# Probabilities and values of an attention kernel as f16 pairs instead of float32r pairs

## The reference, cut to what matters

```python
q = (x @ Wq) ...                                   # 16 heads
k, v = jnp.split(x @ Wkv, 2, axis=-1)              # 4 groups
scores = jnp.einsum('brgtd,bgsd->brgts', qg, k) / jnp.sqrt(jnp.float32(HD))
scores = jnp.where(causal[None, None, None], scores + bias[None], -jnp.inf)
attn = jax.nn.softmax(scores, axis=-1)
out = jnp.einsum('brgts,bgsd->brgtd', attn, v)
return out @ Wo + bo
...
x = x + _L0_attn_ref(xn, ...) + _L0_ffn_ref(xn, ...)
```

## Time and profile before

| | |
|---|---|
| median of 3 runs | 1827.52 us (1823.84 to 1828.0) |
| profiled execution | 1826.36 us, of it the span of the profile 1824.5 us |
| granted TensorE clock, mean | 0.987 |
| TensorE busy | 1742.3 us, 95% |
| TensorE weight loads (beside the matmuls) | 959.6 us, 53% |
| VectorE busy | 1466.6 us, 80% |
| ScalarE busy | 990.1 us, 54% |
| GpSimd busy | 981.4 us, 54% |
| preamble: GpSimd's low parts of the query weights | 23.50 to 28.49 us |
| preamble: remainder of the first projection (L774) | starts 36.16 us |
| preamble: extra rows of the queries, stored by SyncE | 56.71 us |
| main loop: TensorE's first matmul | 116.83 us |
| main loop: ones of `vst` (L1257, two fills) | 124.12 us, 0.98 us |
| main loop: turn of the maxima in slot 3, ten heads apart | 435.62 and 1446.63 us, 101.1 us a head |

### The profile page before, as it was taken

The page is one execution under the profiler, slowest core; times in us unless marked ns, Lnnn a source line. Parts: engine busy times, 40 slices in busy tenths (PEclk is TensorE's granted clock), DMA queues, the critical chain, the costliest instruction groups (busy, mean ns, idle before and its releaser), DMA issues. The chain is left out here.

```text
span 1824.5 us, 26824 instructions
## 1 busy us (share of the span) xinstructions
PE 1742.3 (95%) x8528; PEld 959.6 (53%) x8528; DVE 1466.6 (80%) x2619; ACT 990.1 (54%) x1715; POOL 981.4 (54%) x785
## 2 busy tenths in 40 slices
PE   4979999999999999999999999999999999999948
PEld 3755555555555555555555555555555555555536
DVE  6878788787878787887878787888878787878848
ACT  2435656465656566464656555564646465665620
POOL 4225646374646556474646465563746465564617
PEclk9999999999999999999999999999999999999979
DMA  6860120202020210202020201103020202012073
GB/s 196 221 162 15 42 48 16 66 24 65 24 60 15 66 23 23 67 15 65 25 65 21 65 14 50 40 16 73 17 65 25 63 17 69 14 36 53 16 203 133
DMA packets 113387, 104.65 MB, mean 57 GB/s; under 512 B 61873, under 2 KB 81329, under 8 KB 111457
## 3 DMA queue, kind: packets, MB, share of 16 engines
q1 hardware_dynamic: 113248, 102.93, 21.9%
HBM read 68.03 MB, written 22.02 MB: 49 GB/s over the span
## 5 line engine op out<-in xcount | busy, mean ns | idle before, releaser
L1268 POOL TENSOR_TENSOR plo<-p,phi 128x512 fp32r<-128x512 f32 (+1 forms) x576 | 710.1, 1237 | 362.1 <-ACT phi L1108 360.5
L1102 ACT ACTIVATE p<-score_ps 128x512 f32<-128x512 f32 (+1 forms) x576 | 328.2, 570 | 381.4 <-DVE score_ps L1187 196.0
L1108 ACT ACTIVATE phi<-p 128x512 fp32r<-128x512 f32 (+1 forms) x576 | 350.2, 608 | 15.2
L1275 POOL TENSOR_TENSOR il<-prod,ih 128x512 f16<-128x512 f32 x128 | 156.7, 1224 | 342.4 <-DVE ih L1174 342.4
L1052 PE MATMUL o_ps<-phi,vst 128*96 128x512 f32 (+3 forms) x640 | 328.2, 529 | 0.0
L1035 PE MATMUL score_ps<-qst,kst 128*128 128x512 f32 (+3 forms) x640 | 319.1, 515 | 0.0
L1201 DVE TENSOR_REDUCE mxp<-max_ps 128x1 f32<-128x512 f32 (+2 forms) x320 | 201.9, 631 | 59.8 <-PE max_ps L1010 47.0
L1180 DVE TENSOR_TENSOR acc<-down_ps,acc 128x512 f32<-128x512 f32 x256 | 174.6, 682 | 74.1 <-PE down_ps L984 72.2
L1052 PE MATMUL o_ps<-plo,vst 128*96 128x512 f32 (+3 forms) x640 | 221.2, 362 | 0.0
L1201 DVE TENSOR_REDUCE mxp<-turn_ps 128x1 f32<-128x512 f32 (+3 forms) x320 | 184.7, 577 | 19.7 <-PE turn_ps L1013 7.8
L997 PE MATMUL up_ps<-xh,wh 128*128 128x512 f16 x512 | 199.9, 390 | 0.0
(11 more groups left out here) (158 smaller groups left out, 2807.3 us busy)
## 6 DMA issues: line engine op xcount, KB each, us to landing
qst<-q_parts SPq DMA_DIRECT2D x204, 64.0 KB
kst<-k_parts SPq DMA_DIRECT2D x48, 256.0 KB, 4.1
o<-oraw SPq DMA_DIRECT2D x192, 64.0 KB, 2.0
vst<-v_parts SPq DMA_DIRECT2D x17, 512.0 KB, 6.5
q_parts<-o SPq DMA_DIRECT2D x24, 256.0 KB, 3.4
raw<-L_ffn_gate_W_packed_dram SPq DMA_DIRECT2D x18, 256.0 KB, 3.0
raw<-n_L_ffn_up_W_packed_dram SPq DMA_DIRECT2D x18, 256.0 KB, 3.1
raw<-L_ffn_down_W_packed_dram SPq DMA_DIRECT2D x18, 256.0 KB, 3.9
```

What stands on the lines that cost most here:

```text
L1102: nc.scalar.activation(p32[n % PR][:, 0:cols], score_ps[:, 0:cols], ACT.Exp).then_inc(exp_done, 1)
L1108: nc.scalar.activation(phi[n % PP][:, 0:cols], p32[n % PR][:, 0:cols], ACT.Copy).then_inc(phi_done, 1)
L1268: nc.gpsimd.tensor_tensor(plo[n % PP][:, 0:cols], p32[n % PR][:, 0:cols], phi[n % PP][:, 0:cols].bitcast(F32), ALU.subtract).then_inc(plo_ ...
L1275: nc.gpsimd.tensor_tensor(il[w % 2][:, a, :], prod[a][:], ih[w % 2][:, a, :], ALU.subtract).then_inc(il_done, 1)
```

## The change

`phi`, `plo` and `vst` become f16. So that f16 holds them, the exponential gets a bias of 15 ln 2 (`pshift`, a tile of one column that GpSimd fills at the start of the main loop, and for which ScalarE waits before its first instruction there), and the values are scaled by a power of two (`vscale`) found from the largest value weight; `o_copy` scales back (`oback`). The ones and a block of zeros are now filled once into `vt` in the preamble and stored with the parts, in the order high, ones, low, zeros, so that a value load fills `vst` whole. The value product still uses 96 weight columns. Finding the scale adds to the preamble: two reductions and two small steps on VectorE before the second layer norm, a maximum over partitions on GpSimd between its weights and the extra rows of the keys, and seven small steps on VectorE behind the second layer norm.

```diff
-    v_s = nc.dram_tensor("v_parts", [KVH, P, NT, 2 * HD], F32, kind="Internal").ap()
+    v_s = nc.dram_tensor("v_parts", [KVH, P, NT, 4 * HD], F16, kind="Internal").ap()
...
-            vst = [tile(f"vst{b}", [P, NT, 3 * HD], F32R) for b in range(2)]
+            vst = [tile(f"vst{b}", [P, NT, 4 * HD], F16) for b in range(2)]
...
                     if c == 0:
+                        sp.wait_ge(vt_filled, 2)
...
+                nc.gpsimd.memset(vt[:, :, :, 1, :], 1.0).then_inc(vt_filled, 1)
+                nc.gpsimd.memset(vt[:, :, :, 3, :], 0.0).then_inc(vt_filled, 1)
...
+                pool.wait_ge(vtop_done, 1)
+                nc.gpsimd.partition_all_reduce(vall, vtop, P, RMAX).then_inc(vall_done, 1)
...
+                    if c == 0:
+                        act.wait_ge(vscale_done, 1)
...
-                                         ACT.Copy).then_inc(v_hi, 1)
+                                         ACT.Copy, scale=vscale[:, 0:1]).then_inc(v_hi, 1)
...
+                def value_bound():
+                    wv = wkv[:, :, KVH * HD:]
+                    dve.wait_ge(w_in, 32)
+                    link(nc.vector.tensor_reduce(vmost, wv, AX.X, ALU.max))
+                    link(nc.vector.tensor_reduce(vleast, wv, AX.X, ALU.min))
+                    link(nc.vector.scalar_tensor_tensor(vmost, vleast, -1.0, vmost, ALU.mult, ALU.max))
+                    nc.vector.tensor_reduce(vtop, vmost, AX.X, ALU.max).then_inc(vtop_done, 1)
+
+                def value_scale():
+                    dve.wait_ge(vall_done, 1)
+                    link(nc.vector.tensor_scalar(vall, vall, 1 / LIM, LIM, ALU.max, ALU.min))
+                    link(nc.vector.tensor_scalar(vall.bitcast(I32), vall.bitcast(I32), 0x7F800000, None, ALU.bitwise_and))
+                    link(nc.vector.tensor_scalar(vscale[:].bitcast(I32), vall.bitcast(I32), -1.0, float(254 << 23),
+                                                 ALU.mult, ALU.add))
+                    link(nc.vector.tensor_scalar(vscale[:], vscale[:], VS, None, ALU.mult))
+                    link(nc.vector.memset(oback[:], 1.0))
+                    nc.vector.tensor_scalar(oback[0:HD], vall[0:HD], 1 / VS, None, ALU.mult)
+                    nc.vector.tensor_scalar(oback[2 * HD:3 * HD], vall[2 * HD:3 * HD], 1 / VS, None, ALU.mult
+                                            ).then_inc(vscale_done, 1)
...
                 for k in range(KT):
                     turned_lo(0, k)
+                value_bound()
                 layer_norm(1)
+                value_scale()
...
-        phi = [sb(f"phi{i}", [P, CH], F32R) for i in range(PP)]
-        plo = [sb(f"plo{i}", [P, CH], F32R) for i in range(PP)]
+        phi = [sb(f"phi{i}", [P, CH], F16) for i in range(PP)]
+        plo = [sb(f"plo{i}", [P, CH], F16) for i in range(PP)]
+        pshift = sb("pshift", [P, 1], F32)
...
-                                    o_ps[0:3 * HD, tok:CH], vst[par][:, j, :], src[n % PP][:, col:col + width],
+                                    o_ps[0:3 * HD, tok:CH], vst[par][:, j, 0:3 * HD], src[n % PP][:, col:col + width],
...
+                act.wait_ge(pshift_done, 1)
+
...
-                        nc.scalar.activation(p32[n % PR][:, 0:cols], score_ps[:, 0:cols], ACT.Exp).then_inc(exp_done, 1)
+                        nc.scalar.activation(p32[n % PR][:, 0:cols], score_ps[:, 0:cols], ACT.Exp, bias=pshift[:, 0:1]
+                                             ).then_inc(exp_done, 1)
...
-                        nc.scalar.activation(oraw[c % 2][:], o_ps[0:3 * HD, :], ACT.Copy).then_inc(oraw_done, 1)
+                        nc.scalar.activation(oraw[c % 2][:], o_ps[0:OPARTS * HD, :], ACT.Copy, scale=oback[0:OPARTS * HD, 0:1]
+                                             ).then_inc(oraw_done, 1)
...
-                for b in range(2):
-                    nc.gpsimd.memset(vst[b][:, :, 2 * HD:].bitcast(F32), 1.0).then_inc(ones_done, 1)
+                nc.gpsimd.memset(pshift[:], PSHIFT).then_inc(pshift_done, 1)
```

More of the change, by code:

```diff
@@ L54 @@
 PV_LAG = 3
+OPARTS = 3
+PSHIFT = 15 * math.log(2)
 def score_blocks():
@@ L147, in build @@
         on = sb("on", [P, CH], F32)
-        o3 = [sb(f"o3_{b}", [P, 3, CH], F32) for b in range(2)]
+        o3 = [sb(f"o3_{b}", [P, OPARTS, CH], F32) for b in range(2)]
         oscale = sb("oscale", [P, KT], F32)
+        vscale = sb("vscale", [P, 1], F32)
+        oback = sb("oback", [P, 1], F32)
         wo, *oc = [t[:].rearrange("p k t -> p (k t)").bitcast(F32).rearrange("p (h g n) -> p h g n", h=2, n=CH)[:, h]
@@ L360, in preamble @@
         rmax, rall, rinv = (table(1) for _ in range(3))
+        vmost, vleast = table(KT), table(KT)
+        vtop, vall = table(1), table(1)
         turn = [ctx.enter_context(nc.psum_tensor(f"turn{i}", [P, CH], F32)) for i in range(2)]
@@ L805, in main_loop @@
     q_s, k_s, v_s, aug_s, o_s = (e[n] for n in ("q_s", "k_s", "v_s", "aug_s", "o_s"))
-    xh, xl, acc, ident, identb, mask_ts, mask_st, tab, on = (
-        e[n] for n in ("xh", "xl", "acc", "ident", "identb", "mask_ts", "mask_st", "tab", "on"))
+    xh, xl, acc, ident, identb, mask_ts, mask_st, tab, on, oback = (
+        e[n] for n in ("xh", "xl", "acc", "ident", "identb", "mask_ts", "mask_st", "tab", "on", "oback"))
     wh, wl, cur, qst, kst, vst, o3 = (
@@ L837, in main_loop @@
         nmx = sb("nmx", [P, TPC, NB], F32R)
-        oraw = [sb(f"oraw{i}", [3 * HD, CH], F32) for i in range(2)]
+        oraw = [sb(f"oraw{i}", [OPARTS * HD, CH], F32) for i in range(2)]
         gate_ps, up_ps, turn_ps, max_ps, score_ps, o_ps = (
@@ L941, in gather_o @@
                         sp.wait_ge(on_done, after(i))
-                    for part in range(3):
+                    for part in range(OPARTS):
                         sp.dma_start(o3[par][c * HD:(c + 1) * HD, part, :],
@@ L964, in _ @@
                 for b in range(2):
-                    sp.wait_ge(o_out[b], after(48 * HEADS * NCH // 2))
+                    sp.wait_ge(o_out[b], after(16 * OPARTS * HEADS * NCH // 2))
             @block.tensor
```

47 lines of the change are left out of this document (27 added, 20 removed).

## The result

The changed kernel takes 1803.78 us (median of 4 runs, 1803.24 to 1804.92), the kernel before 1825.68 us in the same comparison (4 runs, 1821.66 to 1828.0): ratio 0.9886, 95% interval 0.9871 to 0.9901. The forecast was 1807, the range 1798 to 1825. The span of the profiled execution goes from 1824.5 to 1801.8 us, 22.7 less; the sum had 20.6. The signs named ahead stand as follows: the ends around phi and plo are 0.216 apart, the load behind them is a matmul ahead, the exponential takes 0.68 us, the waits of the turn are 18.1 us (near 20 expected), the third projection starts at 38.11 (near 38.5), a head takes 99.62 us (99.7).

The account below looks back on a forecast made before the run. TensorE, busy in 95% of the span, was taken as the bound; -16.8 - 8.9 + 3.7 + 0.8 + 1.5 - 0.9 = -20.6 us from 1826.4 gave 1805.8, plus 1.2 for the median: 1807, range 1798 to 1825.

Parts of the forecast that it names:

- The signs named ahead: Values expected in the profile after, for matmul ends, the load behind, exponential, turn waits, third projection and head time.
- The likeliest case: The forecast itself, all terms as summed, 1807 us; chance 0.48.
- phi and plo: Value product: with f16 both take the f16 step, gaining 1.05 us a head, 16.8 us over 16 heads.
- the f16 matmul behind: Behind plo: its load can come forward again, gaining 0.0155 us in 36 blocks, 0.56 us a head, 8.9 in all.
- turns: Turns of the row maxima: exponentials longer by 0.09 us each lengthen the stalls, 0.23 us a head, 3.7 us in all.
- scores: Single score bank: three or so of 36 exponentials hold up the next load, 0.05 us a head, 0.8 us in all.
- preamble: Before the main loop: VectorE's added steps and GpSimd's maximum make TensorE's third projection 1.5 us later.
- start of the loop: Start of the main loop: GpSimd loses two fills, so TensorE resumes 0.9 us earlier after the fill of acc.
- The rule of the Trainium skill: Fast weight load only for 128 non-FP32 columns, so 96 f16 columns would load slowly; cost left to rivals A (0.30), B (0.10).
- the slack of 0.13 us: Scores: 0.24 us from exponential's end to load, less some 0.11 for the signal; just what 0.09 plus 0.05 takes.
- The bound of +5: Preamble's worst case: 5 us lost if nothing shrinks in VectorE's second norm (3.2) and the lower clock lasts longer.
- a stretch at the lower clock less: Start of the main loop: the good bound of that term, -4 us against the -0.9 taken.

Follow-up runs that it names:

- e4: The changed kernel with all 128 columns of the value tile as weights of the value product, the last 32 being zeros; 1804.12 us.
- e2: The kernel before, with a tile of zeros as the exponential's bias and a tile of ones as the output copy's scale; 1829.34 us.
- e7: The changed kernel with the shift of 15 ln 2 added to the negated row maximum, not given as the exponential's bias from a tile; 1800.30 us.
- e3: The kernel before with the search for the value scale added to its preamble, its result unused; 1831.25 us.
- e1: The changed kernel with only the f16 types kept: no exponential bias, no scale search, no scale at the copies; 1795.53 us.
- e5: The changed kernel with VectorE's seven small scale steps moved from before the projection remainders of chunk 0 to before those of chunk 1; 1800.19 us.
- e6: As e5, with the value scale's maximum over partitions taken by a diagonal matrix, a TensorE matmul and a VectorE reduction, not by GpSimd; 1800.57 us.
- e10: As e9, with the maximum for the MLP's scales also moved from GpSimd to TensorE and VectorE; 1781.97 us.
- e11: As e10, with TensorE's matmul for the MLP's maximum and VectorE's steps behind it one projection later; 1775.15 us.
- e12: The kernel before with only one rounded row of maxima turned and subtracted, VectorE's second small step removed; 1804.44 us.
- e9: The changed kernel with the edits of e6 and e7, and only one row of maxima turned, without VectorE's second small step; 1779.05 us.

## Why the prediction was right

The likeliest case came about, by its own steps, with the preamble and the start mis-sized. That the total came within 2.1 us is in part luck, since their errors (+3.1 and -1.7) go against each other. Sizes per head below come from the ends of all of TensorE's matmuls in ten heads of each trace, each step compared with the f16 step for as many columns (512: 0.2155 us).

| term | predicted | measured |
|---|---|---|
| phi and plo, a head | -1.05 | -1.18 |
| the f16 matmul behind, a head | -0.56 | -0.48 |
| turns, a head | +0.23 | +0.21 |
| scores, a head | +0.05 | 0 (what is left: -0.04) |
| a head | -1.33 | -1.49 |
| preamble | +1.5 | +4.56 |
| start of the loop, beyond a head's share | -0.9 | -2.6 |

**The value product** (1.05 predicted). The surplus of a float32r matmul went whole with the type: over ten heads phi had 5.29 us and plo 6.53 over the same matmuls in f16, now both have nothing. That it lay in the stream and not in the float32r load is argued from its growth with the columns (phi's matmuls of 128, 256, 384 and 512 columns take 4, 8, 14 and 15 ns more than in f16); no run has the one without the other. The 0.13 beyond the sum is the part that I left out with the words that the slow load behind a matmul of 128 columns "costs before and after": it does not. The plo of 384 columns behind a phi of 128 had 40 ns over the step, now 1. The load there is 123 ns against 163, but e4, with 98 ns, has 1 as well.
**The matmul behind** (0.56). The decision was right. Of its reason this much is shown: slow f16 loads of 96 columns do not block the next load, and e4, which makes them fast, moves nothing. So the block went with float32r; whether its stream or its load made it was not separated. The size was counted for 36 blocks, but behind some stands a float32r matmul for the maxima, which is as it was. The rule of the Trainium skill weighed there ("TensorE: Matmul & The Clock Gate", Weight-path perf modes) agrees with the traces in that 96 f16 columns load slower than 128 (123 and 98 ns); what it costs here is nothing.
**ScalarE** (+0.28 with the scores). 90 ns were right (594 to 684). The waits of the turns are 18.1 us against "near 20"; the rest of their loss shows as idle time of the loads there (39.3 us before, 43.9 after). e2 has the price without the f16 streams, 0.30, and e7 without the tile, 0.20. That the scores cost nothing says that the slack of 0.13 us was a little more than it looked.
**The preamble** (+1.5 predicted, +4.56 measured) is the failed size. Its first half held: answer at 36.16, third projection at 38.11. (The four steps of the second norm took 1.92 us and not the 2.8 assumed, but VectorE then stood 3.88 us for the answer.) Against the kernel before (37.06 in its trace) that is 1.05 us late; the value part's projection of chunk 1 is 2.81 late (54.35 against 51.54), and its end 4.5 (58.96 against 54.43), which is the whole loss. The step that failed is "GpSimd's way back costs the keys' and queries' extra rows 7 us, which are stored at 56.7 us", put at nothing because the rows themselves are not needed earlier. What it left out is the engine beside them: GpSimd's copies of the rows, now at 43.50 to 50.57, fall on VectorE's small steps of chunk 2's norm and make that norm 2.65 us longer (5.68 against 3.03), and behind TensorE's wait at 54.35 came a stretch at the lower clock (e3: +2.7 with the wait and without that stretch). The bound of +5 covers the size, but was taken for another reason, that nothing shrinks in the second norm.
**The start** (-0.9 predicted, -2.6 measured): the step itself gave 0.6, for TensorE is back from the stall of the fill 16.74 us behind the loop's first matmul and not 17.36; the rest came as the bound named "a stretch at the lower clock less": the lower level fills 5.6 of the 24 us from there on, 9.9 before. GpSimd came back 7.3 us behind TensorE's first matmul (7.0 before), and the fill met less of VectorE's work (the cast is held 3.54 us and not 6.35). This is not owed to the fills removed alone: e2 keeps them and its start is 2.3 us shorter beyond the head's share, e1 lacks them and has 1.9. Nor is it owed to ScalarE's wait: e7 lacks that wait, and its start is 1.1 us shorter still. What decides how much of the work the fill meets stays open.
**The rest** is 2.3 us shorter, of which 1.4 is head 15's own share; of the 0.9 us left, some 0.6 is the clock's by an estimate (the lower level fills 30.7 us of it and not 32.0, at half the speed), and 0.3 stays open.

The sum missed by 2.1 us of 22.7: -2.5 in the heads, +3.1 in the preamble, -1.7 at the start, -0.9 in the rest.

## What to carry to other kernels

When TensorE is the bound, lay the ends of neighbouring matmuls beside the fastest step of the same number of columns, and ask of each surplus whether the stream or the load makes it; the matmul behind counts too. A small reduction over partitions on GpSimd can be paid three times, by the way in, by the way back, and by GpSimd's later work that then falls on VectorE's; where nobody waits for the answer it may cost nothing in the end (e5 against e6). A diagonal and one matmul did the same for 0.14 us, but only where TensorE's operand has long been there (e10 against e11). And before a type is changed for 22 us, read which single instruction stands on the chain at the stalls: one small step less, often held by another engine, was worth about as much (e12).

## What the runs showed of the hardware that I had not expected

GpSimd stands 7.4 to 7.9 us before its maximum over partitions and 7.1 to 7.9 behind it in the preambles of the changed kernel, e3, e4, e5 and e7, though what follows is an ordinary instruction (35.75 and 43.50 above; in e6, without the maximum, the same instruction comes at once, at 28.26). While it does so, VectorE's four steps of 512 elements take 1.92 us instead of 5.38 beside GpSimd's copies, so that its absence makes VectorE's stage faster (third projection at 32.92 in e5). The Trainium skill, "GPSIMD Engine Reference", Instruction dispatch, has about 6 us for the first call of freshly loaded code; the rows have 7.59 on the way in, and 7.37 on the way back, of which that section does not speak.
Whether VectorE's small step of 0.17 us is held by GpSimd's rest of 1.28 in slot 7 is decided by some 10 ns: it is not held where it starts up to 5 ns behind the rest, and is held in all heads, of all kernels here, in which it starts 10 ns or more behind. That decides 1.1 us of the step, 0.18 us of a head in the kernel before and 0.69 us in e9 to e11. Kernels with the same heads differ by up to 0.30 us a head, 5 us in all, by how often it falls either way: a gain of that size needs the per-head times beside it before it is put down to an edit.
A wait of 2 us of TensorE was followed by a stretch at the lower clock in one place (54.35 in the changed kernel, granted 0.66 over 54 to 59) and not in another (138.13, granted 1.00 over 134 to 140). At the same projection of chunk 2, e12 waits 1.92 us and has such a stretch behind it (granted 0.57 over 73 to 77), e11 waits 2.29 us (at 71.85) and has none.
